# A four-layer graph network on one core: tile groups ended inside the last layer's loop, degree sums on VectorE in the first

## What is computed

```
# 1: mean over neighbours
out = (1 / (sum(adj, 1) + beta))[:, None] * (adj @ h + beta[:, None] * h) @ kernel + bias
# 2: softmax over the neighbours of adj * score
out = softmax(where(adj != 0, adj * (h @ H_v).T, -1e30)) @ h
# 3
out = relu(concat([h, adj @ h]) @ W.T + b)
# 4: attention with 4 heads of 32, masked by adj == 0, and a gate
alpha = softmax(where(adj == 0, -inf, q @ k.T / sqrt(32)));  out = alpha @ v
g = sigmoid([out, x_r, out - x_r] @ Wb);  out = g * x_r + (1 - g) * out
```

## Time and profile before

| | us |
|---|---|
| timed runs: median (lowest, highest) | 1197.55 (1195.87, 1203.04) |
| profiled execution, its own time | 1189.68 |
| its span, first to last instruction | 1188.0 |
| busy in the span: PE, DVE, ACT, POOL | 895.1, 822.4, 687.1, 509.9 |
| granted TensorE clock, mean | 0.85 |
| a block of layer 1 in the loop | 47.14 |
| 40 steps of layer 4 | 914.0 to 1152.0 |
| last VectorE instruction ends | 1184.93 |

### The profile page before, as it was taken

The page is one execution under the profiler, slowest core; times in us unless marked ns, Lnnn a source line. Parts: engine busy times, 40 slices in busy tenths (PEclk is TensorE's granted clock), DMA queues, the critical chain, the costliest instruction groups (busy, mean ns, idle before and its releaser), DMA issues.

```text
span 1188.0 us, 25534 instructions
## 1 busy us (share of the span) xinstructions
PE 895.1 (75%) x5768; PEld 569.3 (48%) x5768; DVE 822.4 (69%) x2230; ACT 687.1 (58%) x3070; POOL 509.9 (43%) x526
## 2 busy tenths in 40 slices
PE   4979999999999352666667469997667788888750
PEld 1535555556455221555556334554444555555540
DVE  7388879879788774666665761121655888888788
ACT  4999879987977031434433351000455778888762
POOL 4002767735333434555555401666214444444420
PEclk9999988988989575676665679998897999999985
DMA  9556657657450125444444538984233444444421
GB/s 367 192 207 244 241 205 290 231 203 262 170 188 27 54 86 169 133 134 134 127 121 119 179 109 343 356 290 116 89 126 111 121 116 119 120 123 122 119 72 71
DMA packets 109354, 196.19 MB, mean 165 GB/s; under 512 B 21152, under 2 KB 93088, under 8 KB 103488
## 3 DMA queue, kind: packets, MB, share of 16 engines
q1 hardware_dynamic: 84368, 74.10, 19.8%
q10 hardware_dynamic: 8448, 82.99, 18.0%
q0 software_dynamic: 16432, 37.97, 11.7%
HBM read 166.17 MB, written 25.97 MB: 162 GB/s over the span
## 4 chain that ended last, share of the span: by engine, by line
PE 42%; DVE 22%; issue 17%; ACT 7%; another core or an unknown queue 2%; DVEq 2%; SPq 1%; DMA 1%; POOL 1%; ACTq 0%; POOLq 0%
PE ps L1877 7%; PE ps L1768 7%; PE ps L1852 4%; ACT unread L936 4%; PE ps L1931 4%; DVE work L1265 4%; PE ps L1922 3%; DVE work L1575 3%; PE ps L1794 2%; PE ps L1836 2%; DVE work L1266 2%; PE ps L1720 2%; PE ps L1716 2%; PE ps L1845 1%
## 5 line engine op out<-in xcount | busy, mean ns | idle before, releaser
L936 ACT ACTIVATE unread<-work 128x128 bf16<-128x128 f32 x1024 | 300.7, 295 | 6.9 <-ACT unread L936 2.1
L1768 PE MATMUL ps<-work,h_wide 128*128 128x512 f32 x512 | 241.8, 629 | 17.3 <-ACT h_wide L848 17.3
L936 ACT ACTIVATION_READ_ACCUMULATOR unread<-work 128x1 f32 x1024 | 191.6, 187 | 0.0
L755 POOL DMA_INDIRECT work<-in_adj_rows,adj_stage x120 | 157.3, 1311 | 60.1 <-issue 32.9
L1768 PEld LDWEIGHTS ps<-work,h_wide 128*128 128x128 f32 x512 | 101.3, 203 | 140.3 <-issue 138.6
L797 POOL DMA_INDIRECT work<-h_table,stage x105 | 100.2, 954 | 126.7 <-DMA h_table<-h_wide 59.3
L797 POOL DMA_INDIRECT work<-kv_table,node_flat x93 | 89.1, 958 | 121.7 <-PE ps L1941 77.5
L1575 DVE CUSTOM_DVE_ANT_0 work<-ps,work 128x512 f32<-128x512 f32 x168 | 116.2, 747 | 22.0 <-PE ps L1922 20.0
L1931 PE MATMUL ps<-ident,work 128*128 128x128 f32 x648 | 95.9, 281 | 42.6 <-issue 22.6
L1029 ACT ACTIVATE work<-work 128x512 f32<-128x512 f32 x165 | 117.2, 713 | 11.9 <-DVE work L1584 7.8
L797 POOL DMA_INDIRECT work<-h_table,node_flat x93 | 88.5, 951 | 71.8 <-issue 38.6
(11 more groups left out here) (230 smaller groups left out, 1655.7 us busy)
## 6 DMA issues: line engine op xcount, KB each, us to landing
work<-in_adj_rows ACTq DMA_DIRECT2D x38, 2048.0 KB
work<-adj_table SPq DMA_DIRECT2D x66, 192.0 KB
work<-in_adj_rows SPq DMA_DIRECT2D x6, 2048.0 KB
mask_table<-work SPq DMA_DIRECT2D x43, 128.0 KB
work<-mask_table SPq DMA_DIRECT2D x43, 128.0 KB
work<-kv_table SPq DMA_DIRECT2D x43, 128.0 KB
adj_table<-work SPq DMA_DIRECT2D x42, 128.0 KB
work<-in_adj_rows SPq DMA_DIRECT2D x66, 64.0 KB
```

What stands on the lines that cost most here:

```text
L755: nc.gpsimd.indirect_dma_start(out=ag[:, h, c, :], out_offset=None, in_=adj_rows, in_offset=bass.IndirectOffsetOnAxis(ap=adj_stage[:, h // ...
L936: ins = nc.scalar.activation(unread[:, m % (MQ // 2) * TB + t, :], ring[:, q, m, t * P:(t + 1) * P], ACT.Abs, accum_out=seen[:, b, t, q * ...
L1768: ins = mm(ps[:, 0, :], h_sb[:, q * MQ + m, :], ring[:, q, m, :], start=(q + m == 0), stop=False)
```

## The change

First layer: `reduce_slot` adds the sum of the quarter before to each quarter's sum, so that the last quarter's degp holds the whole block, and TensorE needs 4 products of one column for the degrees in place of 16. These and the products with k0 (`products`) move from the block's end to behind the first quarter of the next block, and so does `places`. The copy of the block's sum to aggT moves into the last quarter's `reduce_slot`, behind its first sum.

Third layer: VectorE works out, for up to 336 quads beyond one per tile, the tile (extra_tile) and the place in the tables (extra_unit).

Fourth layer: quads that aren't a tile's first group come first (one turn of four in a loop and four unrolled), then the first groups of tiles 0 to 31 in order, unrolled on VectorE, ScalarE and SyncE (`Late`, `each_late`). Running maxima are kept per tile in best_tab. SyncE stages the indices of every quad. Groups 0 to 2 of 8 tiles are ended in parts behind the steps of later tiles: outputs at tile 8, 16, 24, products one later, and so on, scalings at the fifth and sixth, the blend at the seventh. SyncE stores groups 0 and 1 from its loop. The diff, cut to its core:

```diff
+        class Late(Quad):
+
+            def __init__(self, turns, k):
+                super().__init__(turns + k // TURN if k // TURN else turns, k % TURN)
+                self.turns, self.k = turns, k
+                self.tile = min(k - TURN, T) if k >= TURN else None
+
+            def ahead(self, n):
+                return Late(self.turns, self.k + n)
...
+        def each_late(eng, body):
+
+            turns = looped_turns3(eng)
+            with eng.Fori(0, turns) as i:
+                for u in range(TURN):
+                    body(Quad(i, u))
+            for k in range(TURN + T):
+                body(Late(turns, k))
+            return turns + T // TURN + 1
 
...
                 def load(g):
                     q, b = g.q + begin, g.b
                     if k == 3:
-                        t = quad_value(sp, quad_tile, q, T)
-                        sp.dma_start(mk[:, b, :], mask_table[bass.ds(q * P, P), :]).then_inc(ac_full[k][b], 16)
+                        if g.tile is None:
+                            unit = quad_value(sp, extra_unit, g.q, QUADS)
+                            t = quad_value(sp, extra_tile, g.q, T)
+                        else:
+                            settle(sp)
+                            unit = sp.value_load(bounds[0:1, g.tile:g.tile + 1], min_val=0, max_val=QUADS)
+                            t = g.tile
+                        sp.dma_start(stage[:, b, :], node_flat[:, bass.ds(GC * unit, GC)]).then_inc(ac_full[k][b], 16)
+                        sp.dma_start(mk[:, b, :], mask_table[bass.ds(unit * P, P), :]).then_inc(ac_full[k][b], 16)
                         sp.dma_start(qs[:, b, :], qT[:, bass.ds(t * P, P)]).then_inc(ac_full[k][b], 16)
-                        return
+                        return T if g.tile is None else g.tile
                     sp.dma_start(ac[:, b, 0:GC, :], adj_table[bass.ds(q * P + P, P), :]
                                  .rearrange("p (c n) -> p c n", c=GC)).then_inc(ac_full[k][b], 16)
...
-                    load_own(Quad(0, b, bufs))
-                steps = sparse_quads(sp, step) if k == 2 else each_quad(sp, step)
+                    load_own(Quad(0, b, bufs), T if k == 3 else None)
+                steps = (sparse_quads(sp, step) if k == 2 else each_quad(sp, step) if k == 1 else
+                         each_late(sp, step))
                 if k == 1:
...
             def reduce_slot(nb, q):
 
                 dve.wait_ge(slot_full[q], 16 * nb + 16 if not isinstance(nb, int) else 16 * (nb + 1))
-                link = Link(dve, link_sum, 2, nb * NQ + q)
+                link = Link(dve, link_sum, 3 if q else 2)
+                link.base = (3 * NQ - 1) * nb + (3 * q - 1 if q else 0)
                 link(nc.vector.tensor_tensor(half_sum, ring[:, q, 0:MQ // 2, :], ring[:, q, MQ // 2:MQ, :], ALU.add))
+                if q == NQ - 1:
+                    dve.wait_ge(agg_done, nb + 1)
+                    nc.vector.tensor_copy(aggT[:, :], ps[:, 0, :]).then_inc(agg_out, 1)
                 link(nc.vector.tensor_tensor(quarter_sum, half_sum[:, 0:MQ // 4, :], half_sum[:, MQ // 4:MQ // 2, :], ALU.add))
+                if q:
+                    dve.wait_ge(slot_summed[q - 1], nb + 1)
+                    settle(dve)
+                    link(nc.vector.tensor_tensor(quarter_sum[:, 0, :], quarter_sum[:, 0, :], degp[:, q - 1, :], ALU.add))
                 link.end()
-                if q == 0:
+                if q == NQ - 1:
                     dve.wait_ge(deg_done, nb + 1)
                 nc.vector.tensor_tensor(degp[:, q, :], quarter_sum[:, 0, :], quarter_sum[:, 1, :],
                                         ALU.add).then_inc(slot_summed[q], 1)
...
+            def extra_tiles(n):
+                some = slice(NX // WAYS * n, NX // WAYS * n + NX // WAYS)
+                shape = [P, NX // WAYS, T]
+                is_past = work[:, 21504:21504 + NX // WAYS * T].rearrange("p (e t) -> p e t", t=T)
+                extra_link(nc.vector.tensor_tensor(is_past, extra_ends[:, :].rearrange("p (a t) -> p a t", a=1).to_broadcast(shape),
+                                                   iota_x[:, some].rearrange("p (e a) -> p e a", a=1).to_broadcast(shape), ALU.is_le))
+                extra_link(nc.vector.tensor_reduce(cap[:, some], is_past, AX.X, ALU.add))
+
+            def extra_units():
+                tiles, units = cap[:, 0:NX], quad_first[:, 0:NX]
+                extra_link(nc.vector.tensor_copy(extra_tile[:, 0:NX], tiles))
+                extra_link(nc.vector.scalar_tensor_tensor(units, tiles, 1.0, iota_x[:, :], ALU.add, ALU.add))
+                extra_link(nc.vector.tensor_scalar(extra_unit[:, :], units, ends[:, T:T + 1], None, ALU.min))
+
+            dve.wait_ge(iotas, 20)
+            extra_link(nc.vector.tensor_tensor(extra_ends[:, :], ends[:, 1:T + 1], iota_x[:, 1:T + 1], ALU.subtract))
+            for n in range(WAYS // 2):
+                extra_tiles(n)
...
                 nc.vector.tensor_scalar(nbest3[:, b, :], best3[:, b, :], -SCALE, None, ALU.mult).then_inc(mx_ready[3], 1)
-                nc.vector.tensor_scalar(capped3[:, (b + 1) % NBUF, :], best3[:, b, :], cap[:, bass.ds(q + 1, 1)], None,
-                                        ALU.min).then_inc(cap_ready, 1)
+                after = capped3[:, (b + 1) % NBUF, :]
+                if g.tile is not None:
+                    nc.vector.tensor_copy(after, best_of(g.ahead(1).tile)).then_inc(cap_ready, 2)
+                    return
+                t, t_after = tile_at(g), tile_at(g.ahead(1))
+                nc.vector.tensor_copy(best_of(t), best3[:, b, :]).then_inc(cap_ready, 1)
+                dve.wait_ge(cap_ready, 2 * q + 3)
+                settle(dve)
+                nc.vector.tensor_copy(after, best_of(t_after)).then_inc(cap_ready, 1)
...
+            def group3(i):
+
+                tiles = slice(FT * i, FT * i + FT)
+                return tiles, fin[:, i % 2, :, :], zed3[:, tiles]
+
+            def outputs3(i):
+                tiles, outs, zeds = group3(i)
+                end_link(nc.vector.reciprocal(rden3[:, tiles, :].rearrange("p t (h a) -> p t h a", a=1), acc3[:, tiles, :, C:C + 1]))
+                end_link(nc.vector.tensor_tensor(outs.rearrange("p t (c h) -> p t h c", h=H), acc3[:, tiles, :, 0:C],
                                                  rden3[:, tiles, :].rearrange("p t (h a) -> p t h a", a=1)
...
+            def products3(i):
+                tiles, outs, zeds = group3(i)
+                end_link(nc.vector.tensor_tensor(prodw, outs, wide_row(wb_bc[:, 0:P]), ALU.mult))
+
+            def gate_sums3(i):
+                tiles, outs, zeds = group3(i)
+                sums = zeds.rearrange("p (t a) -> p t a", a=1)
+                end_link(nc.vector.tensor_reduce(zeds, prodw, AX.X, ALU.add))
+                nc.vector.tensor_tensor(sums, sums, xz[:, tiles, :], ALU.add).then_inc(z_ready, 1)
+
+            def less_skip3(i):
+                tiles, outs, zeds = group3(i)
+                nc.vector.tensor_tensor(outs, outs, xr[:, tiles, :], ALU.subtract)
+
+            def gates3(i):
+                tiles, outs, zeds = group3(i)
+                dve.wait_ge(ez_ready, i + 1)
+                end_link(nc.vector.tensor_scalar(zeds, zeds, 1.0, None, ALU.add))
+                nc.vector.reciprocal(zeds, zeds).then_inc(gate_ready, 1)
+
+            def blend3(i):
+                tiles, outs, zeds = group3(i)
+                dve.wait_ge(scaled, 2 * i + 2)
+                nc.vector.tensor_tensor(x_sb[:, tiles, :], outs, x_sb[:, tiles, :], ALU.add).then_inc(fin_ready, 1)
+
+            def blend_tiles3(i):
+                dve.wait_ge(gate_ready, i + 1)
+                for j in range(FT):
+                    t = FT * i + j
+                    ins = nc.vector.scalar_tensor_tensor(x_sb[:, t, :], fin[:, i % 2, j, :], zed3[:, t:t + 1], x_sb[:, t, :],
+                                                         ALU.mult, ALU.add)
+                ins.then_inc(fin_ready, 1)
+
+            def step_end3(g):
+                step3(g)
+                if g.tile is None or g.tile < FT:
+                    return
+                part = {0: outputs3, 1: products3, 2: gate_sums3, 3: less_skip3, 4: gates3, 7: blend3}
+                if g.tile % FT in part:
+                    part[g.tile % FT](g.tile // FT - 1)
 
...
+            def products(nb, first=False):
+                pe.wait_ge(slot_summed[NQ - 1], nb + 1)
+                for j in range(TB):
+                    ins = mm(ps[:, 6, j:j + 1], degp[:, NQ - 1, j * P:(j + 1) * P], ones[:, 0:1], start=True, stop=True)
+                ins.then_inc(deg_done, 1)
+                if first:
+                    pe.wait_ge(ld, 16 * NLD)
+                pe.wait_ge(up_used, 1 + nb)
+                pe.wait_ge(agg_out, nb + 2)
+                for j in range(TB):
+                    ins = mm(ps[:, 1, j * P:(j + 1) * P], aggT[:, j * P:(j + 1) * P], k0_sb[:, :], start=True, stop=True)
```

(19 more changed lines are left out.)

167 lines of the change are left out of this document (79 added, 88 removed).

## The result

The changed kernel took 1211.61 us in the median of 19 executions (1201.29 to 1218.03), the kernel before, beside it, 1195.87 (19 executions, 1183.97 to 1204.34): ratio 1.0153, interval 1.0131 to 1.0176 (ratios here and below go by the fast executions alone, those at most 1.5% above a kernel's fastest; the two medians divided give 1.0132). Forecast was 1197.0 and no difference. In two later measurements, on two different chips, the same pair gave 1.0055 (1.0021 to 1.0088) and 1.0118 (1.0075 to 1.0161). The changed kernel is slower each time, by 0.5 to 1.5%.

The account below looks back on a forecast made before the run. TensorE and VectorE taking turns bound the first layer; VectorE, closely followed by gathers, the fourth. Layers of -2.6, 0 and +2.0 summed to -0.6 us on a profiled 1189.68, so a median of 1197.0, range 1183 to 1212.

Parts of the forecast that it names:

- (b): First layer: VectorE gets three more sums of 512 columns a block, 0.79 us each, 2.4 us.
- (c): First layer: VectorE's waits for TensorE go, 3.25 us a block; with the added sums 47.14 becomes 46.3, -6 over six blocks.
- (d): End of the first layer: VectorE's list wait of 4.09 us gets 1.7 us shorter.
- (e): First layer: TensorE waits for VectorE's codes and its last quarter comes late, 0.4 us x 6 = +2.4.
- (a): Fourth layer's fill: staging each quad's indices by a third transfer delays the gather, +2.7 us, bounds +1 and +4.
- (b) Early steps: Fourth layer, quads not first in a tile: register loads and table copies cost +5.5 us, 1.2 of it in the fill.
- (c) The next ten steps: Fourth layer: the ten steps after the early ones stay at 6.1 us, the gather's pace.
- (d) Last steps: Fourth layer: the last 24 steps carry three groups' ending work, 164 us instead of 146.8, +17.
- (e) The end: Fourth layer after step 40: only the last group is left, 9.5 us instead of 32.7, -23.2.
- Rival A: First and fourth layers: moved work finds more room than forecast, -24 us at most, half way 1184.5; chance 0.19.
- Rival B: Fourth layer: TensorE's clock falls in four stretched steps of each group, giving 1214 us; chance 0.15.
- Rival C: Fourth layer: staging bounds every step, 6.5 us in the 20 unstretched steps, +8 us, 1205; chance 0.13.

Follow-up runs that it names:

- the pairs: Kernel before and changed kernel traced twice, the second time on a faster chip; the changed kernel's stages together took +19.1 us, then +11.8 us.
- staged_before: Kernel before with SyncE staging the indices of every fourth-layer quad and gathers waiting for all three transfers, in its own order of quads: ratio 0.9995.
- either mend of SyncE's part: Changed kernel with the first three fourth-layer quads' indices staged before the third layer's row stores, ratio 1.0075, or their table values loaded into registers there, 1.0084.

## Why the prediction was wrong

First layer, forecast -2.6, measured +0.7 and +2.4 in the pairs and 3 in the mean over all traces. Right: VectorE takes TensorE's place as the bound, and the sums are the price. Right too: +2.7 for the first two blocks; it is +3.0, all in the second. (b) was a little small, 0.87 us a sum with its wait, not 0.79. The step that failed is (c) and the -6 us made of it. The waits for the fold and the list went, 2.6 us, but of the exposed load, from which I took 0.75, only 0.3 did (1.1 us of "issue" ahead of L1210 before, 0.8 ahead of L1265 now): 47.14 - 2.9 + 2.6 = 46.84, which is what a block takes. And 47.14 us was no measure for all blocks: others of the kernel before take 45.5, and against their mean of 46.9 the changed kernel's 47.0 is no gain at all. (d) gave 0.8 of its 1.7 us. (e), +2.4, cost next to nothing in steady blocks: VectorE waits for no other engine there.

Third layer, forecast 0 with a bound of +2, measured +6.2, +0.8 and a mean of 4.5 on the slower chips. I looked for cover on VectorE, which had it, and not at what its operations do to GpSimd. The row shows the gather of 2.73 us. By the Trainium skill, page SBUF — State Buffer, section "SBUF: two separate sides", a GpSimd instruction that reads SBUF and a VectorE operation with two inputs there lock each other out for the whole instruction. The trace agrees in one direction: L1574 with two inputs holds a gather, L1576 with one doesn't, and a held gather goes on only when L1574 has ended (778.23 against 777.42 here, and so 32 times of 32). The other direction doesn't show: beside a gather that started first L1574 takes 2.02 or 2.03 us as ever. The first three of the six pairs met none, as no gather runs beside them. That this lock makes all of the 4.5 us wasn't tested apart; on the faster chip gathers are stretched too and the dense stretch is at most 0.8 us longer.

Fourth layer, forecast +2.0, measured +5.8 and +12.7. Its start, forecast 2.7 (a) and 1.2: measured +7.1 and +10.1. Of these, +0.7 and +0.1 lie ahead of the last row store's end, +3.5 and +3.4 from there to the first gather, +3.0 and +6.5 from the gather to the first step. (a) was right: with the staging alone (staged_before) the gather is 3.2 us later and the first step 2.3. The 1.2 us for the quad that ends the fill were the failure: its quads pay for their register loads there too, and with the loads moved it is 29.3 us from gather to step instead of 32.2, on the second pair's chip 29.0 instead of 33.3. On that chip the start with the loads moved is still 2.1 us longer than with the staging alone (90.1 against 88.0), which stays unexplained. Nor did either mend of SyncE's part bring anything, which is not settled.

(b) Early steps, forecast +4.3: +8.1 and +9.5. This is the term that failed most, together with the start. I let the two loads and copies (1.25 us) eat the 0.45 us that VectorE waits in a step. They cost 1.8 us, and the copy that they delay is one on which TensorE waits, so the step grew from 6.1 to 8.0 with no cover: the first six steps after the first take 9.4 and 11.4 us more, the nine after them 1.3 and 1.9 less. With the loads moved beside the scores the 15 steps cost +2.7 (93.9 against 91.2) and +1.7 (90.2 against 88.5): that was the lower bound of the term, but this code didn't reach it. What I had not thought of at all is TensorE's clock here: it was granted 1.00 in these steps before and 0.87 after (0.83 in the second pair, with all five steps below 1). PE behind one of the delayed copies:

```profile
965.17 1.12 PE L2033 MATMUL ps<-ident,work 128*128 128x128 f32 x4 [2.47 <-DVE work L1691]
966.22 2.09 PE L2024 MATMUL ps<-work 32*128 32x512 f32 x8
```

The scores take 2.09 us after that wait and 1.14 at the full clock, a step earlier. It isn't the main price, as the steps at 1.00 take 8.07 and 7.58 us and those at 0.72 to 0.86 8.0 to 8.1; what it adds wasn't tested apart.

(c) The next ten steps: right, 5.3 to 6.5 us each. (d) Last steps, forecast +17: +13.0 and +15.5, by place 7.9, 6.6, 6.6, 6.3, 5.9, 5.9, 7.7, 6.5 against 8.0, 7.0, 7.1, 6.8, 6.15, 6.35, 6.35, 6.85. Only the seventh is longer than forecast (7.35 and 6.9 in the other two groups). There ScalarE's four scalings stand ahead of its exponentials, and behind a wait of 1.47 us TensorE falls to the lower clock for part of the step, in timelines of PE and ACT:

```profile
1083.33 1.90 PE L2033 MATMUL ps<-ident,work 128*128 128x128 f32 x8 [1.47 <-ACT work L1078]
```

```profile
1079.42 1.27 ACT L1117 ACTIVATE work<-work 128x128 f32<-128x128 f32 x4
```

(e) The end, forecast -23.2: -22.4.

Rival A: of the 12 us that it takes off (d) 4.0 and 1.5 came, of its 9 in the first layer none. Rival B: its time, 1214, was the nearest, its mechanism not: the clock was 0.98 over the last 24 steps, and below 1 in four of them. Its bound of a third of the steps wasn't reached, so the rule of the Trainium skill quoted there (TensorE: Matmul & The Clock Gate, HAM oscillation) decided nothing in these steps; where the clock did fall step after step is in the early ones, for which B had no price. Rival C fell: staging costs a step nothing. What I had no rival for were small costs on the path in three places at once. (b) with the fill's quads came to 8.1 + 3.0 and 9.5 + 6.5 us, over its bound of 9; the tables passed theirs of 2 on the slower chips; only (a) stayed within 1 to 4.

How much of 1.0153 is the change: the stages give +13 us (1.1%) in the first pair without the 6.4 us of untouched code, and +16 (1.4%) in the second without its -4.1. The kernel before has a median of 1195.87 us in the measurement of 1.0153 and 1207.88 in that of 1.0055, the changed kernel 1211.61 and 1212.74; why it is the kernel before that differs stays open, since no trace of it exists from the latter. On the two chips where both were measured, the two mends together take 19.2 and 18.3 us off the changed kernel, more than its whole loss there (4.9 and 12.7 us by the medians): without the added sums and with the early loads covered the change is a gain.

## What to carry to other kernels

Before work is moved into a loop, price what the move needs (an order, its tables, the loads of its numbers) and not only the work: here the work gained 9 us and its order lost more. Two register loads behind operations of 0.16 us stood on VectorE's path with 1.3 us; behind operations of 0.75 us no gap was left. When one engine hands work to a second to escape a shared bound, read the bound from several rounds of the loop: here one round took 47.14 us, another 45.5, and the forecast was built on the longer.

## What the runs showed of the hardware

The kernel before took 1196 to 1208 us (medians) in four measurements, on three chips at least, and 1132 in a fifth, on another chip. 36 us of that lie in the steps of layer 2 (200 against 164). In the trace from the faster chip a quad takes 3.8 us in the stretch below, and TensorE's eight products take 1.16. In the first trace waits of 5 us come in every few quads, and the products behind them take 2.08, at the lower clock; the fourteen traces from the slower chips have four to eight waits of over 3 us each in the 40 quads, and the four from the faster one have none. PE in the first trace:

```profile
552.41 2.08 PE L1852 MATMUL ps<-work 128*128 128x128 f32 x8 [4.96 <-ACT work L977]
```

and in the second:

```profile
552.58 1.16 PE L1852 MATMUL ps<-work 128*128 128x128 f32 x8 [0.69 <-ACT work L977]
```

In this stretch of the second trace each quad is like the last, with waits of at most 1.1 us; in the first the round falls out of step and pays for it in the clock each time. Why ScalarE's results, on which these products wait, come late on one chip and not on the other, the traces don't say.
